# Perceiver layer in fp32 on one core: the first three tiles of cross attention in another order, with the second tile's context loaded earlier

## The chip, the cores and the metric

The kernel runs on one core of one Trainium2 chip. Time is device microseconds of one execution, and the number compared is the median of several executions. Everything is fp32. The engines in this text are PE (TensorE, matrix products; PEld is its weight load), DVE (VectorE), ACT (ScalarE), POOL (GpSimd) and SP (SyncE, which here only issues DMAs). They run side by side and meet through semaphores; each engine works off its own list of instructions strictly in the order written.

## The reference, cut to what matters

The change touches the first of three parts, a cross attention of 32 batches with 64 query rows each on a context of 1601 rows. The other two parts (causal attention, mixture of experts) are unchanged.

```
def _L0_xattn_ref(encoder_hc, decoder_hq, w_sim, b_sim, W_qv, b_qv):
    w1, w2, w3 = (w_sim[:d], w_sim[d:2 * d], w_sim[2 * d:])
    Sim = (encoder_hc @ w1)[:, :, None] + (decoder_hq @ w2)[:, None, :] + jnp.einsum('bid,bjd->bij', encoder_hc * w3, decoder_hq) + b_sim[0]
    A = jax.nn.softmax(Sim, axis=2)
    hq_hat = jnp.einsum('bij,bjd->bid', A, decoder_hq)
    Batt = jax.nn.softmax(jnp.max(Sim, axis=2), axis=1)
    hc_bar = jnp.einsum('bi,bid->bd', Batt, encoder_hc)[:, None, :]
    hc_hat = jnp.broadcast_to(hc_bar, encoder_hc.shape)
    feats = jnp.concatenate([encoder_hc, hq_hat, encoder_hc * hq_hat, encoder_hc * hc_hat], axis=-1)
    return feats @ W_qv + b_qv
...
x = x + _L0_xattn_ref(_layernorm(x, axis=-1), ctx_1024, ...)
```

## The kernel before

The 2048 rows of x are 16 tiles t of 128 rows; a tile is two batches. For each tile the context of both batches comes from memory twice: transposed, T(t), as four chunks k of two DMAs of 800.5 KB each (`load_ctx_T`, line 339), and by rows, N(t), as four groups q of two DMAs of 768 KB and a rest of two DMAs of 130 KB (`load_ctx_N`, lines 350 and 353). That is about 13.1 MB a tile. Each has one buffer only: chunk k of T(t) is issued when PE has used chunk k of T(t-1) (`sim_done`), group q of N(t) when PE has used group q of N(t-1) (`pv_done`). All loads go through SP's one queue, in the order written.

The work of one tile on PE, with the names in the code:

- `normed_T(t)` (line 1551): transposes of the normed rows. DVE makes the queries `qT` of them (`queries`, line 921).
- `similarities(t)` (line 1590), called sim(t) here: 32 matmuls in four chunks k; chunk k needs chunk k of T(t). The scores fill four banks.
- DVE takes the row maximum of the scores (`maxima`, line 930, then `diag`, line 936), ACT the exponential (line 597).
- `spread_max(t)` (line 1624) and `exp_T(t)` (line 1630): they need `diag` and the exponential.
- `attend(t)` (line 1652): 26 matmuls in groups q of N(t).
- `attended_T(t)` (line 1551), `batch_means(t)` (line 1572): of the attended rows, which DVE scales (`attended`, line 975).
- `features(t)` (lines 1602 and 1605): 8 matmuls with the middle half of `w_qv`; it waits once for `wqv_in`.
- `combined_chunk(t, k)` (line 1613), k = 0 to 3: matmuls with weights that DVE combines from the two outer quarters of `w_qv` (`combined`, line 997, which waits once for `wqv_ends_in`).

There are two orders. The *deep* order (`stage_a(t)`) does attended_T, batch_means and features of tile t-1, then spread_max and exp_T of tile t, normed_T(t+1), attend(t) with the four combined chunks of tile t-1 between its groups, and then sim(t+1). So the features of t-1 stand between sim(t) and spread_max(t). The *early* order (`early_features(t)`), used before for tiles 0 and 1, ends a tile within itself: attended_T(t), batch_means(t), features(t), then sim(t+1) with the combined chunks of tile t between its four chunks, and straight after it spread_max(t+1). Before, the deep order starts with tile 3. DVE and ACT have lists to match.

The rows of x come in groups that `TW`, `TX` and `TY` bound: row block 0 first, then 1 to TW-1 (ahead of N(0)), TW to TX-1 (after N(1)), then two more. `finish_norm` takes a group's statistics to the layer norm's factors: a chain of small DVE steps and a square root on ACT.

Of the kernel before, what the change touches and what calls it, by code (L numbers as in the profile page):

```python
# [42 lines left out]
TX = 7  # L43
TW = 3
TY = (TX + T) // 2
# [8 lines left out]
def perceiver_layer(nc, x, ctx_n, ctx_t, w1, w23, b_sim, w_qv, b_qv, wq, wk, wv, wm, b_qk, bv, bm,  # L54
# [5 lines left out]
    with ExitStack() as stack:  # L60
# [267 lines left out]
        def _(sp):  # L328
# [30 lines left out]
            sp.dma_start(X[:, 1:TW, :], x_v[:, 1:TW, :]).then_inc(x_early, 16)  # L359
            load_ctx_N(0, True)  # L360
            sp.dma_start(row_b[:, :], b_qv.partition_broadcast(P)).then_inc(rows_in, 16)
            sp.dma_start(bqkc[:, :, :], b_qk).then_inc(rows_in, 16)
# [4 lines left out]
            for t in range(1, TX - 1):  # L367
                load_ctx_T(t, False)
                if t == TX - 3:
                    sp.dma_start(X[:, TX:TY, :], x_v[:, TX:TY, :]).then_inc(x_in[0], 16)  # L370
                if t == TX - 2:
                    sp.dma_start(X[:, TY:T, :], x_v[:, TY:T, :]).then_inc(x_in[1], 16)
                load_ctx_N(t, False)
                if t == 1:
                    sp.dma_start(X[:, TW:TX, :], x_v[:, TW:TX, :]).then_inc(x_early, 16)
# [207 lines left out]
        def _(act):  # L583
# [22 lines left out]

            def after_scores(t, i, first=False, more=True, norms=None):
# [14 lines left out]
                nc.scalar.activation(ecol, smx, ACT.Exp, bias=nbmax).then_inc(bexp_ready, 1)  # L622
                if norms is not None:
                    sqrt_of_var(*norms)
                if more:
                    normed_copy(t + 1, 1 - i, first)
# [4 lines left out]

            def stage_a(t, i, more=True, norms=None):
                attended_copy(t - 1)
                exp_scores(t, False)
                after_scores(t, i, more=more, norms=norms)

            sqrt_of_var(0, 0, 1)
            normed_copy(0, 0, True)
            exp_scores(0, True)
            after_scores(0, 0, first=True, norms=(1, 1, TW))  # L640
            stage_a(1, 1)
            stage_a(2, 0, norms=(2, TW, TX))
            for t in range(3, TX - 1):
# [209 lines left out]
        def _(dve):  # L853
# [132 lines left out]

            def combined(t, k, first=False, ahead=2):

                if k > 0:
                    dve.wait_ge(wc_used, (KD - 1) * t + k)  # L990
                else:
                    dve.wait_ge(hbar_ready, t + 1)
                    dve.wait_ge(c_ready, min(t + ahead + 1, T) if isinstance(t, int) else t + ahead + 1)
# [16 lines left out]

            def early_features(t, i, first=False):
                features(t, i)
                combined(t, 0, first, ahead=1)
                other_chunks(t)
                residual_a(t)

            def stage_a(t, i, more=True):
# [5 lines left out]
                combined(t - 1, 0)  # L1023
                batch_max(t, False)
# [23 lines left out]
            attended(0, True)  # L1048
            early_features(0, 0, first=True)
            maxima(1, False)  # L1050
            norm_a(2, False)
            batch_max(1, False)
            exp_copies(1, False)
            queries(2, False)
            batch_weights(1, False)
            attended(1, False)
            early_features(1, 1)
            maxima(2, False)
            batch_max(2, False)
            exp_copies(2, False)  # L1060
            batch_weights(2, False)
            dve.wait_ge(x_early, 32)
            for t in range(TW, TX):
                row_stats(t).then_inc(stats_ready, 1)
            finish_norm(2, TX + 2, TW, TX)
            norm_a(3, False)
            queries(3, False)
            attended(2, False)
            for t in range(3, TX - 2):
# [476 lines left out]
        def _(pe):  # L1546
# [33 lines left out]

            def similarities(t, first, between=None):
                pe.wait_ge(qT_ready, KD * (t + 1))
# [3 lines left out]
                for k in range(KD):  # L1586
# [5 lines left out]
                    last.then_inc(sim_done, 1)  # L1592
                    if between is not None:
                        between(k)

# [38 lines left out]

            def attend(t, i, first=False, alone=False):

                if not first:
                    pe.wait_ge(hq_ready, t)
                for c in range(JC):
# [14 lines left out]
                    if c % 3 == 2 or c == JC - 1:  # L1654
                        last.then_inc(pv_done, 1)
                    if c % 3 == 2 and not alone:
                        combined_chunk(t - 1, 1 - i, c // 3)
# [6 lines left out]

            def early_features(t, first=False):
                attended_T(t, first)
                batch_means(t)
                features(t, first)
                similarities(t + 1, False, between=lambda k: combined_chunk(t, t % 2, k))

            def stage_a(t, i, more=True):

                attended_T(t - 1)
                batch_means(t - 1)
                features(t - 1)
# [11 lines left out]
            exp_T(0)  # L1687
            attend(0, 0, first=True, alone=True)
            normed_T(1, False)
            early_features(0, first=True)  # L1690
            spread_max(1)
            exp_T(1)
            normed_T(2, False)
            attend(1, 1, alone=True)
            early_features(1)
            spread_max(2)
            exp_T(2)
            attend(2, 0, alone=True)
            normed_T(3, False)
            similarities(3, False)  # L1700
            stage_a(3, 1)
            with pe.Fori(2, T // 2 - 1) as n:
                for i in range(2):
# [417 lines left out]
```

## Time and profile before

| | |
|---|---|
| median of 3 runs | 1434.79 us (1433.67 to 1434.84) |
| profiled execution, its own time | 1433.62 us |
| its span, first to last instruction | 1431.9 us |
| PE busy | 1368.9 us, 96% of the span |
| DVE busy | 678.1 us, 47% |
| ACT busy | 303.3 us, 21% |
| moved by DMA | 305.40 MB |
| mean granted PE clock | 0.984 of full |

The cross attention takes the first 610 us, 36 us a tile once it runs evenly. The page cuts the span into 40 slices of 35.8 us; a digit is a busy share in tenths. In the timeline views each line is a run of like instructions, with start, time to the end of the last, engine, line, what it writes and reads, the count, and in brackets how long the engine sat idle before and what ended that. A matmul of these shapes shows as two records, so `x64` at line 1590 are the 32 matmuls of sim(t). Ends of matmuls are modelled, so PE may read as busy through short waits.

### The profile page before, as it was taken

What the parts mean: (1) busy time and instruction counts of PE and PEld (TensorE: products, weight loads), DVE (VectorE), ACT (ScalarE), POOL (GpSimd) and SP (SyncE); (2) the same over time, 40 slices, a digit from 0 to 9 for tenths busy, and PEclk for the clock granted to TensorE, in tenths of its full rate; (3) what the DMA queues carried; (4) which work ended last, traced back from release to release, by engine and by line L of the source; (5) the groups of instructions that cost most, each with busy time, mean ns of one, the idle gap of its engine ahead of it and who ended that gap; (6) DMA issues with size and microseconds to landing.
All of it is one profiled execution on the core that took longest, in us unless ns stands there. A gap on an engine that the chain in (4) does not pass through costs nothing.

```text
span 1431.9 us, 20806 instructions
## 1 busy us (share of the span) xinstructions
PE 1368.9 (96%) x7264; PEld 808.1 (56%) x7265; DVE 678.1 (47%) x1251; ACT 303.3 (21%) x518; POOL 167.6 (12%) x197
## 2 busy tenths in 40 slices
PE   6988999999999999979999999999999999999996
PEld 2333444444444444358888887899884444444573
DVE  3234455544444444457777776675432222222244
ACT  2011111111111111125333334323221111111110
POOL 0100000000000000111311003004310000000065
PEclk9999999999999999989999999999999999999998
DMA  9999999999999999526000001314373322222176
GB/s 367 396 400 400 396 391 395 388 384 365 367 361 363 370 363 361 183 87 266 2 0 0 0 0 60 139 69 176 120 274 91 111 92 84 93 74 73 52 230 189
DMA packets 101534, 305.40 MB, mean 213 GB/s; under 512 B 10065, under 2 KB 30545, under 8 KB 101489
## 3 DMA queue, kind: packets, MB, share of 16 engines
q1 hardware_dynamic: 96368, 288.01, 53.7%
q0 software_dynamic: 5120, 16.78, 3.6%
q8 instruction: 30, 0.49, 0.1%
q14 instruction: 16, 0.12, 0.0%
HBM read 269.62 MB, written 35.13 MB: 213 GB/s over the span
## 4 chain that ended last, share of the span: by engine, by line
PE 46%; DVE 3%; issue 3%; POOL 2%; DMA 2%; ACT 1%; SPq 0%; POOLq 0%; DVEq 0%; ACTq 0%
PE ps L1735 11%; PE ps L2013 9%; PE ps L2000 9%; PE ps L1725 8%; PE ps L1551 3%; PE ps L1771 2%; POOL arena L571 2%; DMA arena<-w2t 1%; PE ps L1754 1%; PE ps L1743 1%; PE ps L1864 1%; POOL idx L567 1%; ACT arena L585 0%; DMA moe_in<-arena,idx 0%; PE ps L1613 0%
## 5 line engine op out<-in xcount | busy, mean ns | idle before, releaser
L585 ACT ACTIVATE arena<-ps 128x512 f32<-128x512 f32 x155 | 90.6, 597 | 608.0 <-PE ps L1551 311.8
L1652 PE MATMUL ps<-arena 128*64 128x512 f32 (+1 forms) x832 | 192.0, 597 | 0.0
L1590 PE MATMUL ps<-arena 128*64 128x512 f32 (+1 forms) x1024 | 179.9, 506 | 4.2 <-DVE arena L921 2.9
L1735 PE MATMUL ps<-split 128*128 128x256 f32 x1344 | 171.1, 287 | 1.2 <-DVE split L1092 1.2
L1735 PEld LDWEIGHTS ps<-split 128*128 128x128 f32 x1344 | 165.1, 193 | 6.4 <-issue 5.6
L997 DVE SCALAR_TENSOR_TENSOR arena<-arena,hbar 128x512 f32<-128x512 f32 x128 | 91.9, 759 | 109.3 <-PE ps L1613 105.2
L2013 PE MATMUL ps<-arena 128*128 x312 | 140.4, 592 | 1.2 <-DMA arena<-w2t 1.2
L2000 PE MATMUL ps<-arena 128*128 x312 | 140.4, 593 | 0.4 <-DVE arena L1375 0.4
L1590 PEld LDWEIGHTS ps<-arena 128*64 128x64 f32 x1024 | 66.2, 138 | 130.3 <-issue 122.6
L1652 PEld LDWEIGHTS ps<-arena 128*64 128x64 f32 (+1 forms) x832 | 58.6, 138 | 113.6 <-issue 113.2
L2013 PEld LDWEIGHTS ps<-arena 128*128 128x128 f32 x312 | 59.0, 190 | 75.2 <-issue 75.2
L1725 PE MATMUL ps<-split 128*128 128x512 f32 x384 | 96.0, 399 | 0.7 <-DVE arena L1153 0.7
L1375 DVE STREAM_TRANSPOSE arena<-arena 128x512 uint32<-128x512 uint32 x39 | 27.7, 711 | 134.6 <-PE ps L2000 116.2
L930 DVE TENSOR_REDUCE small<-ps 128x1 f32<-128x1601 f32 x16 | 29.2, 1823 | 127.4 <-PE ps L1590 127.4
L2000 PEld LDWEIGHTS ps<-arena 128*128 128x128 f32 x312 | 56.2, 190 | 56.8 <-issue 56.8
L1725 PEld LDWEIGHTS ps<-split 128*128 128x128 f32 x384 | 69.8, 188 | 17.9 <-issue 2.7
L1551 PE MATMUL ps<-ident,arena 128*128 128x128 f32 x368 | 56.3, 287 | 23.4 <-DVE arena L884 12.2
L495 POOL COPY arena<-arena 128x512 f32<-128x512 f32 x16 | 10.8, 673 | 517.7 <-PE ps L1572 512.4
L1613 PE MATMUL ps<-arena 128*64 128x512 f32 x256 | 66.9, 601 | 4.6 <-DVE arena L997 4.6
L1481 DVE COPY arena<-ps 128x512 f32<-128x512 f32 x39 | 27.0, 691 | 85.6 <-PE ps L2013 85.6
L1725 PE MATMUL ps<-split_ws,split 128*128 128x512 f32 x288 | 67.2, 392 | 0.0
L1551 PEld LDWEIGHTS ps<-ident,arena 128*128 128x128 f32 x368 | 44.0, 147 | 30.7 <-DVE arena L975 11.7
(175 smaller groups left out, 1549.9 us busy)
## 6 DMA issues: line engine op xcount, KB each, us to landing
arena<-ctx_t SPq DMA_DIRECT2D x128, 800.5 KB, 13.7
arena<-ctx_n SPq DMA_DIRECT2D x128, 768.0 KB, 9.2
moe_in<-arena SPq DMA_DIRECT2D x3, 3328.0 KB, 24.0
arena<-moe_in SPq DMA_DIRECT2D x156, 64.0 KB, 1.9
moe_out<-arena SPq DMA_DIRECT2D x39, 256.0 KB, 2.1
arena<-w1t SPq DMA_DIRECT2D x1, 7168.0 KB, 23.1
arena<-ctx_n SPq DMA_DIRECT2D x32, 130.0 KB
arena<-w2t SPq DMA_DIRECT2D x4, 1024.0 KB
```

What stands on the lines that cost most here:

```text
L571: nc.gpsimd.indirect_dma_start(y01[k][i], None, moe_out, bass.IndirectOffsetOnAxis(ap=idx[k][i][:, :], axis=0)).then_inc(y01_in[i], 16)
L585: return nc.scalar.activation(o, i, ACT.Copy)
L930: v.reduce_max(smax, ps[:, 0:4, :].rearrange("p a b -> p (a b)")[:, 0:J], AX).then_inc(max_ready, 1)
L997: v.scalar_tensor_tensor(Wc[:, h, :], w_qv_sb[:, 3 * KD + k, :], hbar[:, k, h:h + 1], w_qv_sb[:, k, :], ALU.mult, ALU.add).then_inc(wc_rea ...
L1551: last = nc.tensor.transpose(dst[:, P * k:P * (k + 1)], src[:, P * k:P * (k + 1)], ident[:, :])
L1590: last = mm(bank(n)[S * h:S * (h + 1), 0:w], qT[:, k, S * h:S * (h + 1)], ctxT[h][:, k, at_j:at_j + w], start=(k == 0), stop=(k == KD - 1))
L1613: last = mm(bank(5)[r, :], F1[i][:, k, r], Wc[:, h, :], start=False, stop=(k == KD - 1))
L1652: last = mm(bank(7)[S * h:S * (h + 1), :], ET[0:w, c, S * h:S * (h + 1)], ctxN[h][0:w, c, :], start=(c == 0), stop=(c == JC - 1))
L1725: last = mm(dst, lhs[a][:, k, :], rhs[b][:, k, :], start=(k + i == 0), stop=(k == n - 1 and i == 2))
L1735: last = mm(dst[:, 2 * P * m:2 * P * (m + 1)], w[a][:, k, c], tokens[b][:, k, :], start=(k + i == 0), stop=(k == KD - 1 and i == 2))
L2000: m1 = mm(bank(2), xgT[:, k, :], w1_sb[:, bass.ds(e, 1), k, :].rearrange("p o f -> p (o f)"), start=(k == 0), stop=(k == KD - 1))
L2013: m2 = mm(bank(3), interT[:, k, :], w2_of(e, k), start=(k == 0), stop=(k == KD - 1))
```

## The change

Three things are changed, together.

1. **Loads.** T(1) is issued right after N(0), ahead of `row_b`, `bqkc` and the three DMAs of `w_qv` (4 MB in all). Before, it came behind them.
2. **Order.** `early_features` is gone on PE and DVE. After attend(0) and normed_T(1), sim(1) follows at once, and the deep order runs from tile 1 on.
3. **Rows of x.** TW is 4 instead of 3: the early group is row blocks 1 to 3 (ahead of N(0)), the next is 4 to 6 and is issued after N(2), where before 3 to 6 was issued after N(1). The square root of that group on ACT and the norm on DVE come after stage_a(2).

```
-TW = 3
+TW = 4
...
             load_ctx_T(0, True, 1, KD)
             sp.dma_start(X[:, 1:TW, :], x_v[:, 1:TW, :]).then_inc(x_early, 16)
             load_ctx_N(0, True)
+            load_ctx_T(1, False)
             sp.dma_start(row_b[:, :], b_qv.partition_broadcast(P)).then_inc(rows_in, 16)
...
             for t in range(1, TX - 1):
-                load_ctx_T(t, False)
+                if t > 1:
+                    load_ctx_T(t, False)
...
                 load_ctx_N(t, False)
-                if t == 1:
+                if t == 2:
                     sp.dma_start(X[:, TW:TX, :], x_v[:, TW:TX, :]).then_inc(x_early, 16)
...
-            after_scores(0, 0, first=True, norms=(1, 1, TW))
+            after_scores(0, 0, first=True)
             stage_a(1, 1)
-            stage_a(2, 0, norms=(2, TW, TX))
+            stage_a(2, 0)
+            sqrt_of_var(2, TW, TX)
...
-            early_features(0, 0, first=True)
-            maxima(1, False)
-            norm_a(2, False)
...
-            early_features(1, 1)
...
+            stage_a(1, 1, second=True)
+            stage_a(2, 0)
             dve.wait_ge(x_early, 32)
             for t in range(TW, TX):
                 row_stats(t).then_inc(stats_ready, 1)
             finish_norm(2, TX + 2, TW, TX)
-            norm_a(3, False)
-            queries(3, False)
-            attended(2, False)
...
-            attend(0, 0, first=True, alone=True)
+            attend(0, 0, first=True)
             normed_T(1, False)
-            early_features(0, first=True)
-            spread_max(1)
-            exp_T(1)
-            normed_T(2, False)
-            attend(1, 1, alone=True)
-            early_features(1)
-            spread_max(2)
-            exp_T(2)
-            attend(2, 0, alone=True)
-            normed_T(3, False)
-            similarities(3, False)
-            stage_a(3, 1)
-            with pe.Fori(2, T // 2 - 1) as n:
+            similarities(1, False)
+            stage_a(1, 1, second=True)
+            with pe.Fori(1, T // 2 - 1) as n:
                 for i in range(2):
                     stage_a(2 * n + i, i)
```

How the instructions stand. First SP's queue from the early rows of x on, before:

```order
L359 DMA arena<-x 128x2x512
L350 DMA arena<-ctx_n 128x1536 x8
L353 DMA arena<-ctx_n 65x512 x2
L361 DMA row_b<-b_qv 128x512
L362 DMA bqkc<-b_qk 128x8
L364 DMA arena<-w_qv 128x8x512
L365 DMA arena<-w_qv 128x4x512
L366 DMA arena<-w_qv 128x4x512
L339 DMA arena<-ctx_t 128x1601 x8
```

and in the change, where the line numbers differ by one or two:

```order
L359 DMA arena<-x 128x3x512
L350 DMA arena<-ctx_n 128x1536 x8
L353 DMA arena<-ctx_n 65x512 x2
L339 DMA arena<-ctx_t 128x1601 x8
L362 DMA row_b<-b_qv 128x512
L363 DMA bqkc<-b_qk 128x8
L365 DMA arena<-w_qv 128x8x512
L366 DMA arena<-w_qv 128x4x512
L367 DMA arena<-w_qv 128x4x512
```

The eight DMAs of T(1) have passed the five of the features' weights and biases; N(1) follows in both. Next PE's list from attend(0) on, before (line 1652 attend, 1551 transposes, 1572 batch means, 1602 and 1605 features, 1590 similarities, 1613 combined chunks):

```order
L1652 MATMUL ps<-arena 64x512 x26
L1551 MATMUL ps<-ident,arena 128x128 x8
L1572 MATMUL ps<-arena 128x128 x4
L1602 MATMUL ps<-arena 128x512 x4
L1605 MATMUL ps<-arena 128x512 x4
L1590 MATMUL ps<-arena 64x512 x6
L1590 MATMUL ps<-arena 64x65 x2
L1613 MATMUL ps<-arena 64x512 x2
...
L1624 MATMUL ps<-arena,ones 128x128
L1630 MATMUL ps<-ident,arena 128x128 x12
```

and in the change (there 1633 is attend, 1534 the transposes, 1573 similarities, 1555 batch means, 1583 and 1586 features, 1605 spread_max, 1611 exp_T, 1594 combined chunks):

```order
L1633 MATMUL ps<-arena 64x512 x26
L1534 MATMUL ps<-ident,arena 128x128 x4
L1573 MATMUL ps<-arena 64x512 x6
L1573 MATMUL ps<-arena 64x65 x2
...
L1534 MATMUL ps<-ident,arena 128x128 x4
L1555 MATMUL ps<-arena 128x128 x4
L1583 MATMUL ps<-arena 128x512 x4
L1586 MATMUL ps<-arena 128x512 x4
L1605 MATMUL ps<-arena,ones 128x128
L1611 MATMUL ps<-ident,arena 128x128 x12
```

Batch means and features of tile 0 have moved from before sim(1) to between sim(1) and spread_max(1); the combined chunks of tile 0 now stand within attend(1). Last DVE's list after it has scaled the attended rows of tile 0, before (979 and 984 features, 997 combined weights, 930 row maximum, 945 batch maximum):

```order
L979 COPY hbar<-ps 128x8
L984 TENSOR_TENSOR arena<-arena 128x512
L997 SCALAR_TENSOR_TENSOR arena<-arena,hbar 128x512 x8
L1007 TENSOR_TENSOR arena<-arena,ps 128x512
L887 BN_STATS stats<-arena 128x6
L930 TENSOR_REDUCE small<-ps 128x1
```

and in the change (933 row maximum, 982 and 987 features, 887 the normed rows of the next tile, 1000 combined weights, 948 batch maximum, 967 a copy of the transposed exponentials):

```order
L933 TENSOR_REDUCE small<-ps 128x1
...
L982 COPY hbar<-ps 128x8
L987 TENSOR_TENSOR arena<-arena 128x512
L887 TENSOR_SCALAR arena<-arena,rstd,nmr 128x512
L916 SCALAR_TENSOR_TENSOR arena,small<-arena,row_a 128x512
L1000 SCALAR_TENSOR_TENSOR arena<-arena,hbar 128x512 x2
L948 TENSOR_REDUCE small<-ps 64x1 x2
L950 TENSOR_SCALAR small<-small 128x1
L967 COPY arena<-ps 128x512
```

The row maximum of tile 1 now comes ahead of tile 0's features, and the first combined weights, which wait for the last of `w_qv`, have the batch maximum and the copies of tile 1 queued behind them.

## Rows read from the trace of the kernel before

**Rows 1.** The page, 40 slices: busy share of the DMA engines, GB/s moved.
```profile
DMA  9999999999999999526000001314373322222176
GB/s 367 396 400 400 396 391 395 388 384 365 367 361 363 370 363 361 183 87 266 2 0 0 0 0 60 139 69 176 120 274 91 111 92 84 93 74 73 52 230 189
```

**Rows 2.** Stretches: length, busy PE, PEld, DVE, ACT, POOL; PE clock, DMA share, GB/s.
```profile
82.00:116.00 34.00, 33.15 (x158) 12.51 (x154) 9.43 (x16) 1.19 (x2) 2.79 (x2) 1.00 1.02 401
116.00:126.00 10.00, 5.65 (x23) 3.81 (x23) 5.44 (x13) 4.10 (x10) 0.00 (x0) 0.66 1.02 354
...
320.00:360.00 40.00, 40.00 (x207) 16.86 (x205) 16.43 (x33) 5.05 (x11) 1.84 (x2) 1.00 0.98 370
```

**Rows 3.** Timeline of PE, tiles 0 to 3 (start, length, what, idle before).
```profile
40.04 0.14 PEld L1652 LDWEIGHTS ps<-arena 128*64 128x64 f32 x2 [0.43 <-DMA arena<-ctx_n]
...
43.86 0.65 PE L1551 MATMUL ps<-ident,arena 128*128 128x128 f32 x4
46.91 1.11 PE L1551 MATMUL ps<-ident,arena 128*128 128x128 f32 x4 [2.39 <-DVE arena L975]
...
64.51 2.92 PE L1590 MATMUL ps<-arena 128*64 128x512 f32 x16 [0.15 <-DMA arena<-ctx_t]
...
68.42 2.92 PE L1590 MATMUL ps<-arena 128*64 128x512 f32 x16
...
76.08 0.49 PE L1624 MATMUL ps<-arena,ones 128*128 128x128 f32 x2 [3.88 <-DVE arena L936]
...
119.98 0.80 PE L1624 MATMUL ps<-arena,ones 128*128 128x128 f32 x2 [3.88 <-DVE arena L936]
...
138.17 11.00 PE L1590 MATMUL ps<-arena 128*64 128x512 f32 x64 [1.46 <-DVE arena L921]
```

**Rows 4.** Timeline of PE in the even part, tiles 3 to 5, deep order.
```profile
159.58 2.79 PE L1652 MATMUL ps<-arena 128*64 128x512 f32 x12
162.21 1.03 PE L1613 MATMUL ps<-arena 128*64 128x512 f32 x4
...
174.23 10.95 PE L1590 MATMUL ps<-arena 128*64 128x512 f32 x64
...
210.24 10.95 PE L1590 MATMUL ps<-arena 128*64 128x512 f32 x64
```

**Rows 5.** DMA issues by line: issue ns, first to last start; time to landing.
```profile
L364 SPq DMA_DIRECT2D arena<-w_qv x1: 1606/1606/1606, 26.2 to 26.2; - x1
DMA to landing us min/median/max: 21.0/21.0/21.0
...
L366 SPq DMA_DIRECT2D arena<-w_qv x1: 2923/2923/2923, 37.7 to 37.7; - x1
DMA to landing us min/median/max: 15.0/15.0/15.0
...
L339 SPq DMA_DIRECT2D arena<-ctx_t x2: 795/1389/1983, 82.1 to 84.1; - x2
DMA to landing us min/median/max: 19.5/20.0/20.5
...
L339 SPq DMA_DIRECT2D arena<-ctx_t x2: 633/800/968, 115.3 to 116.0; - x2
DMA to landing us min/median/max: 19.5/20.6/21.7
...
L339 SPq DMA_DIRECT2D arena<-ctx_t x3: 452/587/1106, 219.2 to 222.1; - x3
DMA to landing us min/median/max: 19.9/20.5/21.5
```

**Rows 6.** PE groups by form, from 10 to 16 us, then from 19 to 23 us.
```profile
L1590 PE MATMUL ps<-arena 128*64 128x512 f32 x14 | 6.2, 1032 | 1.5 <-DVE arena L921 1.5
...
L1590 PE MATMUL ps<-arena 128*64 128x512 f32 x14 | 3.5, 606 | 1.0 <-DMA arena<-ctx_t 1.0
```

**Rows 7.** Timeline of DVE at the end of sim(3).
```profile
149.22 1.82 DVE L930 TENSOR_REDUCE small<-ps 128x1 f32<-128x1601 f32 x1 [10.19 <-PE ps L1590]
```

More of the change, by code:

```diff
@@ L605, in normed_copy, with after_scores @@
                 copy(F1[i].rearrange("p a b -> p (a b)"), bank(4)).then_inc(F1_ready, 1)
-            def after_scores(t, i, first=False, more=True, norms=None):
+            def after_scores(t, i, first=False, more=True):
                 for g in (0, 2):
@@ L622, in after_scores @@
                 nc.scalar.activation(ecol, smx, ACT.Exp, bias=nbmax).then_inc(bexp_ready, 1)
-                if norms is not None:
-                    sqrt_of_var(*norms)
+                if first:
+                    sqrt_of_var(1, 1, TW)
                 if more:
@@ L630, in attended_copy, with stage_a @@
                 copy(F2.rearrange("p a b -> p (a b)"), bank(5)).then_inc(F2_ready, 1)
-            def stage_a(t, i, more=True, norms=None):
+            def stage_a(t, i, more=True):
                 attended_copy(t - 1)
                 exp_scores(t, False)
-                after_scores(t, i, more=more, norms=norms)
+                after_scores(t, i, more=more)
             sqrt_of_var(0, 0, 1)
@@ L985, in features, with combined @@
                                 F2.rearrange("p a b -> p (a b)"), ALU.mult).then_inc(F3_ready, 1)
-            def combined(t, k, first=False, ahead=2):
+            def combined(t, k, first=False):
                 if k > 0:
@@ L992, in combined @@
                     dve.wait_ge(hbar_ready, t + 1)
-                    dve.wait_ge(c_ready, min(t + ahead + 1, T) if isinstance(t, int) else t + ahead + 1)
+                    dve.wait_ge(c_ready, min(t + 3, T) if isinstance(t, int) else t + 3)
                 if first:
@@ L1009, in residual_a, with stage_a @@
                 row_stats(t).then_inc(stats_ready, 1)
[L1011 to L1017, printed above, removed]
+            def stage_a(t, i, second=False, more=True):
                 maxima(t, False)
@@ L1022, in stage_a @@
                     norm_a(t + 1, False)
-                combined(t - 1, 0)
+                combined(t - 1, 0, second)
                 batch_max(t, False)
@@ L1048, in _ @@
             attended(0, True)
-            early_features(0, 0, first=True)
-            maxima(1, False)
-            norm_a(2, False)
[L1052 to L1056, printed above, removed]
-            early_features(1, 1)
[L1058 to L1061, printed above, removed]
+            stage_a(1, 1, second=True)
+            stage_a(2, 0)
             dve.wait_ge(x_early, 32)
@@ L1579, in attended_T, with similarities @@
                 transposes(bank(5), hq).then_inc(hqT_done, 1)
-            def similarities(t, first, between=None):
+            def similarities(t, first):
                 pe.wait_ge(qT_ready, KD * (t + 1))
@@ L1592, in similarities @@
                     last.then_inc(sim_done, 1)
-                    if between is not None:
-                        between(k)
             def features(t, first=False):
@@ L1633, in exp_T, with attend @@
                         last.then_inc(et_done, 1)
-            def attend(t, i, first=False, alone=False):
+            def attend(t, i, first=False):
                 if not first:
@@ L1655, in attend @@
                         last.then_inc(pv_done, 1)
-                    if c % 3 == 2 and not alone:
+                    if c % 3 == 2 and not first:
                         combined_chunk(t - 1, 1 - i, c // 3)
@@ L1663, in normed_T_b, with stage_a @@
                 transposes(bank(i), h1[i]).then_inc(h1T_done, 1)
[L1665 to L1673, printed above, removed]
+            def stage_a(t, i, second=False, more=True):
+                attended_T(t - 1, second)
                 batch_means(t - 1)
-                features(t - 1)
+                features(t - 1, second)
                 spread_max(t)
```

## The prediction

> **What bounds the kernel now.** I read the page's slices first: over the first sixteen the DMA engines are at nine tenths or more, at 360 to 400 GB/s [rows 1]. PE is at nine as well, so the question is which of the two ends last, and where. The stretches tell: from 82 to 116 us the DMA share is 1.02 at 401 GB/s, and only at 320 us does it fall to 0.98 at 370 [rows 2]. Until then transfers are never idle, so they are behind what the free buffers would allow, and a landing can only come earlier if bytes ahead of it in the queue go away. Then the timeline of PE: in the even part sim(4) starts at 174.23 and sim(5) at 210.24, 36.0 us apart, with no idle time, and a sim takes 10.95 [rows 4]; so from the end of a sim to the start of the next is 25.1. There PE is the bound: a tile is 13.1 MB, and at 401 GB/s that is 32.7 us. Before 138 us PE has holes: 2.39 for the scaled rows, twice 3.88 for `diag` straight after a sim, 1.46 for the queries, and smaller ones [rows 3], and after such holes the clock is low (0.66 from 116 to 126 us, [rows 2]). The first three tiles thus have spare PE time, but the transfers set a floor under them.
>
> One rule of the Trainium skill would settle the case otherwise. The rows show 401 GB/s over 34 us [rows 2]. The page "DMA: Bandwidth & Descriptors", section "Where 436 GB/s comes from", says that for transfers from HBM to SBUF the HBM side, about 358 GB/s for a core, binds. By that a tile would take an estimated 36.6 us, transfers would bound all sixteen and no order of PE could gain; the trace goes above it, so I go by the trace.
>
> **The change, part by part.** *Order, on PE alone.* The matmuls are the same ones. After attend(0) and normed_T(1), which ends at 44.5 [rows 3], the queries cost 1.5 as at 138.17, and sim(1) could start at 46.0. With 36.0 a tile, sim(3) would start at 118.0 instead of 138.17: 20 us less. This is the gain if all data were there. The two holes of 3.88 vanish because batch means and features of the tile before (over 7 us) stand between the sim and spread_max, as in the even part, where DVE's maximum runs under them. The hole of 2.39 is covered by sim(1).
>
> *Loads: T(1).* The last large piece of N(0) lands at about 40.0, where a weight load of attend(0) waited for it [rows 3]. The last of `w_qv` lands at 37.7 + 15.0 = 52.7, its middle half at 26.2 + 21.0 = 47.2 [rows 5]. So biases and `w_qv` hold the queue 12.7 us, the part up to the middle half 7.2. T(1)'s chunks 2 and 3 were computed as they landed, at 64.5 and 68.4 [rows 3]; they are 3.9 us apart (1.64 MB, so 418 GB/s). In the change T(1) has 12.7 us less ahead of it, and 0.6 more for the extra row block of x (256 KB at 418 GB/s). Its last chunk lands at 68.4 - 12.7 + 0.6 = 56.3, the others at 44.5, 48.4 and 52.4. A chunk's matmuls take 2.8, so sim(1) ends at 59.1 instead of 57.0. Issue does not hold it: T(1) needs only that sim(0) has used the buffers, over by 25.5, while N(0) still streams until 40.
>
> *Loads: the weights.* The middle half of `w_qv` lands at 56.3 + 7.2 = 63.5, the ends at 69.0. PE wants it for features(0) at about 60.6 (sim(1) end, transposes, batch means), so there is a new hole of 3 us, features end at 70.5 and attend(1) starts at about 73. On DVE the first combined weights wait until 69.0; behind them stand batch maximum and copies of tile 1, which PE's exp_T feeds only from 70.7, so that wait costs nothing. POOL's bias add waits for `row_b`, landing before 60, ahead of the copy that it owes at 60.6.
>
> *Loads: N(1) and T(2).* The bytes ahead of N(1) are the same plus one row block of x, so it lands 0.6 later than before. T(2)'s last chunk landed at 84.1 + 20.5 = 104.6 [rows 5]; before it stood a group of four row blocks of x, 1 MB or 2.5 us, which now comes after N(2). So T(2)'s last chunk lands at 104.6 + 0.6 - 2.5 = 102.7, and its chunks come 3.9 apart, from 91.0. N(1) was complete about 15.7 + 2.5 before 104.6, at 86.4, now 87.0; attend(1) and its combined chunks run at 3.8 a group against a landing every 3.9 and end near 90. So sim(2) starts at 91.0, is paced by the transfers, and ends at 102.7 + 2.8 = 105.5. On PE alone it would have ended at 93: 12 us of the 20 are lost here, and this is the step that sets the gain.
>
> *T(3) and later.* From there 36.0 a tile: sim(3) ends at 141.5. T(3)'s last chunk lands at 116.0 + 21.7 = 137.7 [rows 5], unchanged, since three row blocks of x are behind N(2) and one ahead of N(0), together the same bytes; that floor would be 140.5, just under. N(2), 1.9 earlier than before, is wanted later than it lands. Before, sim(3) ended at 149.1. The gain is 149.1 - 141.5 = 7.6 at sim(3). Is it kept? Later tiles are wanted 7.6 earlier while landing no earlier. The tightest I found is T(6): its last chunk lands at 222.1 + 21.5 = 243.6 at most [rows 5], and sim(6), at 210.24 + 36.0, wants it at 254.5. 10.9 of slack against 7.6: no wait. From 320 us on transfers wait for buffers, so they move with PE, and what follows the cross attention waits for PE.
>
> *Norms.* The statistics and the norm of the second group of rows now come on DVE after attended(2), some 4 us of work, against a wait of 10.19 for the end of a sim at that point [rows 7]: hidden, with 5 us to spare until maxima(3). ACT's square root goes with it, and is over before attended_T(2) needs ACT.
>
> **Sum**, against the profiled execution's own 1433.62: minus 7.6 gives 1426.0. That run is 1.2 below the median of the three, 1434.79; from the median it is 1427.2, which I give.
>
> **What the traces do not show** is PE's clock in the new stretch. Half speed shows as 1032 ns for a matmul of 592 to 606 [rows 6]. What speaks against trouble: in sim(0), from 19 to 23 us, PE waited 1.0 us for a chunk of the same size and its matmuls took 606 ns, having sped up from 1032 while it was paced by the same transfers. So waits of 1.1 us in sim(2) should leave the clock up. The hole of 3 us ahead of features(0) is like those of 2.39 and 3.88 and should bring half speed; the features then last up to 3 us longer, which N(1)'s landings mostly hide. A low stretch after 105.5 would not be hidden: 3.4 us cost 1.5, the 6.8 of 116 to 126 (0.34 of 10 us, doubled) [rows 2] cost 2.9. Below, the bound is nothing.
>
> The Trainium skill's page "TensorE: Matmul & The Clock Gate", section "HAM oscillation — how this bites in real kernels", describes kernels whose every group of matmuls starts at half speed since a DMA wait precedes it; sim(2) has that form. The trace's sim(0) disagrees, so the rule gets a small chance, as the last rival.
>
> **The rivals.** *A, one or two low-clock stretches after 105.5*: 1.5 to 2.9 later, 1428.7 to 1430.1. For it: before, each hole over 2 us had one. Against it: none is expected there.
> *B, T(2) lands earlier than I read* and T(3) is the floor: sim(3) ends at 140.5, a gain of 8.6, 1426.2.
> *C, transfers don't bind* and the PE sum holds: 1414.6. Only if the queue had gaps before; a share of 1.02 says no.
> *D, most is lost*: a low clock from 105.5 on and T(2) landing 2 later, because the weights' rows, moved next to N(1), slow its transfer; 1431.9 to 1434. Nothing shows it.
> *E, slower: PE at half speed through the paced stretch.* Attend(1) with its chunks takes 14.7, sim(2) 10.95; at 1032 against 592 they take 25.6 and 19.1. From a start at 79, sim(2) ends at 123.7 and the kernel at 1445. It decides where half speed adds over 12 us of matmul time (4.5 of slack in sim(2), plus 7.6), so if it lasts for some 28 us on end; the longest seen here is 6.8.
>
> **Chances.** Forecast (1425.5 to 1428.5) 0.55, A 0.22, B 0.07, C 0.03, D 0.08, E 0.05. Forecast, A and B hold 0.84; the range is 1425.0 to 1430.8. A change within 0.2%, 2.9 us, can't be told from none here: faster 0.87, same 0.08, slower 0.05.
>
> **What would show it.** Right: no idle time of 3.88 before spread_max of tiles 1 and 2; a hole of about 3 us before features(0), ended by `w_qv`; four starts about 3.9 apart in sim(2), the last at 102.7; sim(3) from 130.6 to 141.5; none idle after. Wrong: the last chunk of T(2) at another time than 101.5 to 104; PE waiting for T(4) to T(8); matmuls of 1032 ns after 105; sim(3) following sim(2) by other than 36.0.

## The result and the profile after

The changed kernel takes 1422.49 us (median of 4 executions, 1419.65 to 1425.44) against 1434.36 for the kernel before (4, 1433.67 to 1434.84). The ratio is 0.9917, with a 95% interval of 0.9896 to 0.9939: 0.8% faster, 11.9 us. The forecast was 7.6 us, 1427.2 with a range from 1425.0: right in direction, too small in size, and the time is outside the range. Over all sessions, this one included, 22 executions of the changed kernel have a mean of 1423.0 and 56 of the kernel before one of 1433.7, so the gain is better put at 10.7 us.

The page of the changed kernel (its profiled execution took 1425.44), span and the slices that answer to [rows 1]:

```profile
span 1423.7 us, 20826 instructions
...
DMA  9999999999999999336000001414373322222176
GB/s 366 393 398 394 394 394 399 402 401 392 380 368 366 364 367 367 139 106 250 1 0 0 0 0 61 149 60 178 119 274 94 116 90 88 89 73 74 52 229 192
```

What is new is that transfers stay above 390 GB/s from the second slice through the tenth, before only through the seventh: PE asks for its data earlier, and the transfers are behind for longer. Now PE's timeline for tiles 0 to 3, against [rows 3] (line 1534 transposes, 1573 similarities, 1583 features, 1633 attend):

```profile
45.37 0.66 PE L1534 MATMUL ps<-ident,arena 128*128 128x128 f32 x4
47.48 5.61 PE L1573 MATMUL ps<-arena 128*64 128x512 f32 x32 [1.46 <-DVE arena L924]
...
57.47 2.92 PE L1573 MATMUL ps<-arena 128*64 128x512 f32 x16 [1.01 <-DMA arena<-ctx_t]
...
63.74 3.67 PE L1583 MATMUL ps<-arena 128*128 128x512 f32 x8 [1.87 <-DMA arena<-w_qv]
...
73.42 2.79 PE L1633 MATMUL ps<-arena 128*64 128x512 f32 x12 [0.50 <-DMA arena<-ctx_n]
...
85.99 2.79 PE L1633 MATMUL ps<-arena 128*64 128x512 f32 x12 [1.49 <-DMA arena<-ctx_n]
...
91.12 2.91 PE L1573 MATMUL ps<-arena 128*64 128x512 f32 x16 [0.61 <-DMA arena<-ctx_t]
94.95 2.92 PE L1573 MATMUL ps<-arena 128*64 128x512 f32 x16 [0.92 <-DMA arena<-ctx_t]
98.86 2.92 PE L1573 MATMUL ps<-arena 128*64 128x512 f32 x16 [1.00 <-DMA arena<-ctx_t]
103.22 2.92 PE L1573 MATMUL ps<-arena 128*64 128x512 f32 x16 [1.44 <-DMA arena<-ctx_t]
...
131.20 10.96 PE L1573 MATMUL ps<-arena 128*64 128x512 f32 x64
```

The two waits of 3.88 are gone. From 45 us on every wait that is left, but for the queries, ends with a transfer: features(0) waits for `w_qv` until 63.74 (forecast 63.5), sim(2) is computed chunk by chunk as T(2) lands, from 91.12 (91.0) to the last chunk at 103.22 (102.7), and sim(3) starts at 131.20 (130.6), where before it was 138.17: 7.0 us. The stretches (columns as in [rows 2]) show PE's clock on this way:

```profile
46.00:106.00 60.00, 49.12 (x244) 19.80 (x243) 18.54 (x38) 6.93 (x13) 3.10 (x3) 1.00 1.03 399
106.00:142.00 36.00, 36.00 (x185) 15.38 (x180) 19.68 (x44) 6.54 (x13) 1.84 (x2) 1.00 1.02 394
```

The clock is whole throughout the paced stretch, and from 106 on PE is never idle until the end of the cross attention. The norm on DVE was hidden as forecast: DVE's wait for the end of sim(3), 10.19 before [rows 7], is still 5.55.

```profile
142.26 1.83 DVE L933 TENSOR_REDUCE small<-ps 128x1 f32<-128x1601 f32 x1 [5.55 <-PE ps L1573]
```

So the profile shows the 7.6 that was forecast as 7.0, and the median says 11.9. That gap was the first thing to explain.

To see where time goes after sim(3), the matmuls of two profiles can be laid side by side by their order, since the same 7264 records are there. Both kernels were profiled several times for this (below). Mean of nine profiles of the kernel before and of six of the changed one, in us; the borders are times of the kernel before's first profile:

| stretch | before | changed | difference |
|---|---|---|---|
| start to sim(3) | 139.65 (138.1 to 140.9) | 131.18 (130.5 to 131.7) | -8.5 |
| to 605, rest of cross attention | 466.9 | 466.9 | 0.0 |
| to 641, its last tile and the change to attention | 35.65 | 36.35 | +0.7 |
| to 870, attention | 229.0 | 229.0 | 0.0 |
| to 924, its end | 53.73 | 52.02 | -1.7 |
| to 1100, shared experts | 175.7 | 175.1 | -0.6 |
| to 1380, experts | 279.7 | 279.7 | 0.0 |
| to 1400 | 19.66 | 18.13 | -1.5 |
| to the end | 31.31 | 33.02 | +1.7 |
| span | 1431.3 | 1421.4 | -9.9 |

The three dense stretches, to 605, to 870 and to 1380, agree within 0.1 us in all fifteen profiles. PE never waits in the first and the third, and in the second only at its start, for 0.7 and 1.2 us. All scatter sits in the other stretches, which have the holes. From sim(3)'s start to the end the spans are 1288.0 to 1293.7 before and 1288.8 to 1292.5 in the changed kernel. Their means differ by 1.4, which so few profiles do not set clear of that scatter; the 8.5 is clear of it.

### The profile page after: what moved, and what is told of

The parts are those of the page before. It is cut to its first block, busy times and chain, and to the rows that moved or that the text cites. A ratio compares the mean times of both kernels' runs of the same rounds, so it can differ in the third digit from the quotient of the medians.

```text
span 1423.7 us, 20826 instructions
## 1 busy us (share of the span) xinstructions
PE 1364.4 (96%) x7264; PEld 804.4 (57%) x7265; DVE 677.8 (48%) x1251; ACT 303.2 (21%) x518; POOL 164.5 (12%) x197
## 4 chain that ended last, share of the span: by engine, by line
PE 48%; DVE 3%; issue 2%; POOL 2%; DMA 1%; ACT 1%; POOLq 0%; SPq 0%; DVEq 0%; ACTq 0%
PE ps L1700 11%; PE ps L1965 9%; PE ps L1978 9%; PE ps L1690 9%; PE ps L1534 3%; PE ps L1736 2%; POOL arena L573 1%; PE ps L1719 1%; PE ps L1708 1%; PE ps L1829 1%; DMA arena<-moe_out,idx 1%; POOL idx L569 1%; ACT arena L587 0%; PE ps L1594 0%; DMA moe_in<-arena,idx 0%
## 5 line engine op out<-in xcount | busy, mean ns | idle before, releaser
L1583 PE MATMUL ps<-arena 128*128 128x512 f32 x128 | 59.3, 607 | 1.9 <-DMA arena<-w_qv 1.9
```

What stands on the lines that cost most here:

```text
L1583: mm(bank(5), F2[:, k, :], w_qv_sb[:, KD + k, :], start=(k == 0), stop=False)
```

## Experiments

**Is the floor set by T(2)'s landing?** Two kernels change only what is ahead of it in the queue. The first puts the group of three row blocks back:

```
                 load_ctx_N(t, False)
-                if t == 2:
+                if t == 1:
                     sp.dma_start(X[:, TW:TX, :], x_v[:, TW:TX, :]).then_inc(x_early, 16)
```

> One size changed: the group of three row blocks of x (768 KB, 1.9 us at 418 GB/s) is issued after N(1), ahead of T(2), instead of after N(2). Theory 'floor' (the landing of T(2)'s last chunk sets the end of sim(2), and all later tiles follow 36.0 apart): the last chunk is computed from 105.1 instead of 103.2, sim(3) ends at 144.0 instead of 142.1, and the kernel is 1.9 us slower than the changed kernel. Rival 'PE or DVE sets it' (the hole ahead of the features, or the waits within attend(1)): nothing moves, 0 us.

Measured: 1425.14 median (6 executions), ratio to before 0.9940 (0.9926 to 0.9955), 2.6 above the changed kernel timed beside it (1422.55; 1.9 was expected). Its PE timeline:

```profile
93.95 2.91 PE L1573 MATMUL ps<-arena 128*64 128x512 f32 x16 [2.45 <-DMA arena<-ctx_t]
...
105.62 2.92 PE L1573 MATMUL ps<-arena 128*64 128x512 f32 x16 [1.01 <-DMA arena<-ctx_t]
133.60 10.95 PE L1573 MATMUL ps<-arena 128*64 128x512 f32 x64
```

The last chunk is at 105.62; in the changed kernel's profile from the same session it is at 103.71, and sim(3) at 131.69. Both moved by 1.9, which is 768 KB at 418 GB/s.

The second leaves two thirds of N(1)'s large groups out, so what it computes is not the reference's result:

```
-                            sp.dma_start(ctxN[h][:, n * q:n * (q + 1), :],
-                                         main[:, n * q:n * (q + 1), :]).then_inc(ctxN_in[q], 16)
+                            w = 1 if isinstance(t, int) and t == 1 else n
+                            sp.dma_start(ctxN[h][:, n * q:n * q + w, :],
+                                         main[:, n * q:n * q + w, :]).then_inc(ctxN_in[q], 16)
```

> N(1) is loaded only to a third (one of three columns of each large group; attend(1) then reads rows of tile 0 for the rest, so its output is not the reference's): 4.2 MB fewer ahead of T(2), 10 us. Theory 'floor': T(2) is no longer late, sim(2) starts when attend(1) ends, about 88, and ends at 99; sim(3) ends at 135, 7 us before the changed kernel's, and the kernel is 7 us faster, since T(3) lands earlier by the same 10 us. Rival 'transfers don't bind': sim(3) ends at 142 as in the changed kernel.

Measured: 1415.13 (4 executions), 7.4 below the changed kernel. Its PE timeline (line 1574 is the similarities):

```profile
87.25 10.96 PE L1574 MATMUL ps<-arena 128*64 128x512 f32 x64
...
123.28 10.95 PE L1574 MATMUL ps<-arena 128*64 128x512 f32 x64
```

Sim(2) runs through in 10.96 without a wait, and sim(3) starts 8.4 earlier; features(0) still wait 1.87 for `w_qv`. Together they settle that step: T(2)'s landing is the floor of the first three tiles, and what moves it moves sim(3), and the kernel by about as much (1.9 and 2.6, 8.4 and 7.4), until PE is the bound.

**What is the early T(1) worth, and can it stand alone?** One kernel takes it back and keeps the rest:

```
             load_ctx_N(0, True)
-            load_ctx_T(1, False)
...
             for t in range(1, TX - 1):
-                if t > 1:
-                    load_ctx_T(t, False)
+                load_ctx_T(t, False)
```

> One part undone: T(1) again behind biases and w_qv, the deep order and the groups of x as in the change. Sim(1) then waits for T(1): its last chunk is computed from about 69 and ends at 72, features end at 80.5, attend(1) runs from 82.5 to 97, sim(2) from 97 to 108 on PE's pace, T(2) landing at 103. Theory 'floor': sim(2) ends at 108 instead of 106, sim(3) at 144, so the early T(1) is worth only 2 to 3 us of the gain, and this kernel is still 5 us faster than the kernel before. Rival 'the early T(1) is the gain': it is as slow as the kernel before.

Measured: 1426.48 (4 executions), 3.9 above the changed kernel and 8.1 below the kernel before, ratio 0.9940 (0.9925 to 0.9956). Its PE timeline (line 1571 is the similarities):

```profile
58.20 7.08 PE L1571 MATMUL ps<-arena 128*64 128x512 f32 x32 [12.30 <-DMA arena<-ctx_t]
...
97.83 10.95 PE L1571 MATMUL ps<-arena 128*64 128x512 f32 x64
...
133.84 6.42 PE L1571 MATMUL ps<-arena 128*64 128x512 f32 x36
```

Sim(1) waits 12.30 for T(1), yet sim(3) starts only 2.2 later than in the changed kernel's profile of the same session (131.69): sim(2), from 97.83, no longer waits for T(2) and ends at 108.8, where the paced one ends at 106.6. Most of the gain is thus the order, with the rows of x placed as in the change, and 2 to 4 us of it are the early T(1). The order with the rows of x where they were before was not run.

The other kernel has the kernel before's order and only the early T(1):

```
             load_ctx_N(0, True)
+            load_ctx_T(1, False)
...
             for t in range(1, TX - 1):
-                load_ctx_T(t, False)
+                if t > 1:
+                    load_ctx_T(t, False)
```

> One part alone: T(1) ahead of biases and w_qv, with the order and the groups of x of the kernel before. Features(0) then waits for the middle half of w_qv until 63 us (before: 49.5) and sim(1) with its four combined chunks runs after it, from 70 to 86 us (before: 57 to 72), attend(1) until 106, sim(2) with its chunks until 130, attend(2) until 149. Theory 'floor and order belong together': sim(3) starts at 150 to 153, the kernel is 12 to 15 us slower than before, 1447 to 1450. Rival 'the early T(1) helps by itself': sim(3) starts no later than 138, and the kernel is not slower.

Measured: 1446.79 (4 executions) against 1432.4 for the kernel before in that session, ratio 1.0102 (1.0085 to 1.0119): 14.4 slower. Its PE timeline (line 1604 features, 1626 spread_max, 1592 similarities):

```profile
64.14 6.29 PE L1604 MATMUL ps<-arena 128*128 128x512 f32 x8 [13.84 <-DMA arena<-w_qv]
...
92.11 0.49 PE L1626 MATMUL ps<-arena,ones 128*128 128x128 f32 x2 [3.88 <-DVE arena L938]
...
154.04 11.01 PE L1592 MATMUL ps<-arena 128*64 128x512 f32 x64 [1.46 <-DVE arena L923]
```

In that order features(0) stands ahead of sim(1), and all of PE's work waits for `w_qv`. After that wait of 13.84 the first matmuls of features(0) also run at half speed, in 6.29 where the changed kernel needs 3.67. Sim(3) starts a microsecond later than the 150 to 153 expected. The load order and the instruction order have to match; the early T(1) alone is a loss.

**Is the hole ahead of the features free?** The last variant puts T(1) between the two parts of `w_qv`:

```
             load_ctx_N(0, True)
-            load_ctx_T(1, False)
             sp.dma_start(row_b[:, :], b_qv.partition_broadcast(P)).then_inc(rows_in, 16)
...
             sp.dma_start(w_qv_sb[:, KD:3 * KD, :], w_qv_v[:, KD:3 * KD, :]).then_inc(wqv_in, 16)
+            load_ctx_T(1, False)
             sp.dma_start(w_qv_sb[:, 0:KD, :], w_qv_v[:, 0:KD, :]).then_inc(wqv_ends_in, 16)
```

> T(1) stands between the two parts of w_qv: biases and the middle half first, then T(1), then the outer quarters; all else as in the change, and the bytes ahead of N(1) and T(2) are the same. Features(0) has its weights when sim(1) ends, so the hole of 1.9 to 3 us ahead of it is gone, but sim(1) waits for T(1) and ends at 67 instead of 61. Theory 'floor': attend(1) starts at 77 instead of 74, ends at 92, and sim(2) is still paced by T(2): sim(3) starts at 131 to 132 and the kernel is within 1 us of the changed kernel. Rival 'PE's work ahead of attend(1) counts': sim(3) starts 5 us later.

Measured: 1423.98 (4 executions), ratio 0.9928 (0.9910 to 0.9946), within the changed kernel's own scatter. Its PE timeline:

```profile
53.31 10.89 PE L1573 MATMUL ps<-arena 128*64 128x512 f32 x48 [7.45 <-DMA arena<-ctx_t]
64.97 2.92 PE L1573 MATMUL ps<-arena 128*64 128x512 f32 x16 [0.77 <-DMA arena<-ctx_t]
69.20 3.66 PE L1583 MATMUL ps<-arena 128*128 128x512 f32 x8
92.94 5.66 PE L1573 MATMUL ps<-arena 128*64 128x512 f32 x32
...
103.51 2.92 PE L1573 MATMUL ps<-arena 128*64 128x512 f32 x16 [0.99 <-DMA arena<-ctx_t]
...
131.50 3.72 PE L1573 MATMUL ps<-arena 128*64 128x512 f32 x20
```

The features have no wait and start 5.5 later than in the changed kernel; sim(3) starts 0.3 later. What PE does before attend(1) can slip by 5 us for nothing.

**Where is the rest of the gain?** The changed kernel again, unaltered, in five rounds:

> The changed kernel again, unaltered, for the part of the gain that its first profile doesn't hold: 8.2 us there, while two further executions were 13 to 15 us below the kernel before. Theory 'clock': what is over 7 us comes from stretches at half PE clock that fall differently from execution to execution after 599 us; then span and granted clock of the executions lie on one line, about 0.5 us of span for each 1 us of low clock (0.001 of mean clock is 1.4 us of low clock, 0.7 us of span), and times spread from 1419 to 1426 without a step. Rival 'transfers': some executions had T(2) land earlier; then the profile shows sim(3) ending at 137 instead of 142 in a fast execution, and the mean clock doesn't tell the spans apart.

Measured: 1422.55 (5 executions) against 1434.61 (11), ratio 0.9916 (0.9903 to 0.9928). Sim(3) starts at 131.69, 0.5 later than in the first profile, though the span, 1422.1, is 1.6 shorter. So no early landing of T(2) makes the fast executions, and the rival 'transfers' falls. 'Clock' holds only roughly: the executions' mean clocks, 0.989 to 0.992, do not order their times. What was still unknown was how typical the kernel before's one profile is. Three further ones:

> The kernel before, unaltered, a second profiled execution (its first started sim(3) at 138.2 us, span 1431.9). What is open: the changed kernel's two profiles start sim(3) at 131.2 and 131.7, 7.0 and 6.5 us earlier, and keep that to 605 us, but the medians are 12.1 apart. Theory 'first part': the kernel before starts sim(3) later than 138.2 in most executions, 140 to 144, because the matmuls after its holes run at half clock for longer or shorter, and my one profile was a lucky one. Theory 'later part': sim(3) starts at 138 within 0.6 in each, and the other 5 us lie after 605 us, in the stretches at half clock after holes that both kernels have (at 613, 900, 1385, 1415 us).

> The kernel before, a third profiled execution. 'First part': sim(3) starts at 140 to 144. 'Later part': at 138 within 0.6, and the shift of 2 to 3 us against other executions arises at 613 to 634 or at 890 to 905 us.

> The kernel before, a fourth profiled execution, the same two readings: sim(3) at 140 to 144, or at 138 within 0.6.

Measured: sim(3) starts at 139.96, 138.40 and 140.49, after a first 138.17. So neither reading is right alone, and 'first part' is nearer: the start varies by over 2 us, and my one profile was at the short end. Then both kernels side by side on one chip, the changed one in five rounds (after_3), with one more profile of it (after_4) and two of before (before_5, before_6):

> The changed kernel, unaltered, on the chip on which two executions of the kernel before are profiled beside it. By the profiles so far sim(3) starts at 138.2, 140.0, 138.4 and 140.5 us in the kernel before (mean 139.3) and at 131.2 and 131.7 in the changed one: 7.8 us. The medians taken side by side are 12 apart. Theory 'start of before': what lacks lies in the kernel before's first 140 us, whose holes are followed by more or less half clock; beside this kernel's median its profiles show sim(3) at 141 or later. Theory 'later part': from sim(3)'s start to the end the changed kernel needs less than the kernel before, by 3 us or more (so far: 1290.4 to 1292.5 against 1287.9 to 1293.7, no difference). Theory 'the medians of before on that chip were high': here the medians are 8 to 10 apart.

> The kernel before, a fifth profile, beside the changed kernel. 'Start of before': sim(3) from 141 us or later; 'later part': sim(3) from 138 to 140.5 and then 1292 us or more to the end.

> The changed kernel, a further profile. Both theories: sim(3) from 131 to 132, since the landing of T(2) sets it and not the clock; 'later part': 1289 us or less from there to the end.

> The kernel before, a sixth profile, with the same two readings as the fifth.

Measured: 1423.90 (5 executions) against 1433.83 (9), ratio 0.9933 (0.9918 to 0.9947), 9.9 us. Sim(3) starts at 131.19 and 130.45 in the changed kernel, at 139.83 and 138.10 in the one before; the rest of the span is 1289.1 and 1290.4 against 1293.0 and 1290.8. Sim(3) is not at 141, and the later part differs by under 3 on the mean, so the first two theories fail as stated. The third one's reading came, medians 8 to 10 apart: part of the first 12 was the scatter of the medians. Last, three more of before (before_7 to before_9) and two of the changed kernel (after_5, and after_6 in five rounds):

> The kernel before, a seventh profile. Theory 'scatter': sim(3) starts between 138 and 141, and the rest of the span is 1288 to 1294, around 1292; with the eighth and ninth the mean of the whole goes up towards the 1432.0 of all executions. Theory 'later part': the rest is 1292 or more in each of the new profiles of before, and 1290 or less in each of the changed kernel.

> The changed kernel, a fifth profile: sim(3) starts at 130.5 to 131.7. 'Scatter': the rest lies anywhere in 1288 to 1293. 'Later part': 1290 or less.

> The kernel before, an eighth profile, the same readings as the seventh.

> The changed kernel, a sixth profile and five rounds against the kernel before. 'Scatter': the rest after sim(3)'s start is anywhere in 1288 to 1293, and the medians are 9 to 12 apart. 'Later part': 1290 or less.

> The kernel before, a ninth profile. 'Scatter': rest anywhere in 1288 to 1294. 'Later part': 1292 or more.

Measured: after_6 1423.46 (6 executions) against 1434.08 (11), ratio 0.9928 (0.9911 to 0.9945). Sim(3) of before at 140.36, 140.87 and 140.67, of the changed kernel at 131.25 and 131.30. Rest of the span: 1293.0, 1291.7 and 1292.8 against 1290.1 and 1288.8. The medians are 10.6 apart. All of this lies where 'scatter' has it. 'Later part' is missed, by 0.3 in before_8 and by 0.1 in after_5, which is too little to rule out that a small difference is real.

Much of what makes the first part of the kernel before long or short is visible in its stretches. The same ten microseconds around the first wait of 3.88, in the first profile and then in before_7:

```profile
75.00:85.00 10.00, 8.14 (x39) 5.08 (x41) 5.45 (x19) 4.45 (x10) 0.00 (x0) 0.83 1.03 368
```

```profile
75.00:85.00 10.00, 7.51 (x30) 4.94 (x31) 6.39 (x19) 4.46 (x10) 0.00 (x0) 0.66 1.02 368
```

A clock of 0.83 against 0.66: half speed (1.2 GHz) for 3.4 us in the one, for 6.8 in the other. The nine profiles fall in two groups by it. The three with 3.4 us (the first, before_3 and before_6) start sim(3) at 138.10 to 138.40, the six with 6.8 us at 139.83 to 140.87. In before_7:

```profile
140.36 10.03 PE L1590 MATMUL ps<-arena 128*64 128x512 f32 x56 [1.46 <-DVE arena L921]
```

This stretch is not all of it. The wait itself ends at 76.08 in the first profile and at 76.79 on the mean of nine, so 0.7 of the 1.5 us by which the first profile is early are there already. Of the six late profiles, four (before_2, 5, 7 and 9) have 10.2 us of half speed ahead of that wait instead of 6.8. The other two (before_4 and before_8) have no more of it than the early ones, but sim(1) waits for chunks of T(1), up to 1.03 and 1.52 us: there the transfers were late, not the clock.

In the changed kernel the stretches at half speed that occur between 46 and 69 us cost nothing. In after_5 there were two of them, behind attend(0) and behind the hole for `w_qv`:

```profile
46.00:106.00 60.00, 51.73 (x243) 20.64 (x243) 18.26 (x38) 6.94 (x13) 3.10 (x3) 0.94 1.03 401
```

and sim(3) started at 131.25, against 131.20 with the clock whole.

The second piece is at the end of attention. Before_7, then after_6, at the same matmuls:

```profile
892.25 0.63 PE L1551 MATMUL ps<-ident,arena 128*128 128x128 f32 x4 [1.60 <-DVE arena L884]
893.57 0.66 PE L1551 MATMUL ps<-ident,arena 128*128 128x128 f32 x4 [0.69 <-DVE arena L884]
...
900.33 1.11 PE L1551 MATMUL ps<-ident,arena 128*128 128x128 f32 x8 [2.02 <-DVE arena L884]
902.99 1.12 PE L1551 MATMUL ps<-ident,arena 128*128 128x128 f32 x4 [1.54 <-DVE arena L1180]
903.89 1.92 PE L1743 MATMUL ps<-ident,arena 128*128 128x128 f32 x8
```

```profile
882.98 1.31 PE L1534 MATMUL ps<-ident,arena 128*128 128x128 f32 x8 [1.53 <-DVE arena L887]
...
890.12 1.11 PE L1534 MATMUL ps<-ident,arena 128*128 128x128 f32 x8 [1.74 <-DVE arena L887]
892.78 0.66 PE L1534 MATMUL ps<-ident,arena 128*128 128x128 f32 x4 [1.54 <-DVE arena L1163]
893.27 1.04 PE L1708 MATMUL ps<-ident,arena 128*128 128x128 f32 x8
```

After the last hole, 1.54 in both, the same transposes take 1.12 in the one and 0.66 in the other. All nine profiles of the kernel before have a stretch at half speed near there (seven at 900, two at 892 us), but only two of the changed kernel's six. In the changed kernel alone the stretch to 924 takes 51.5 us without it and 52.9 and 53.4 with it. But the clock is not all of the 1.7 us of the table, for the holes ahead differ too. The wait of 0.69 is in all nine profiles of the kernel before and in none of the changed kernel's, and the one of 2.02, in the seven, is 1.74 or 1.75 in all six. With half speed at the same place (the seven, and after) the changed kernel is 0.7 us shorter. The change touches no instruction there; the waits end with DVE's norms, and why those come earlier was not tested. In the kernel before sim(3) starts 12.3 to 13.0 us after the end of the last low stretch in all nine profiles, while in the changed kernel the transfers place it; whether that is why the later holes meet the clock otherwise was not tested either. Both stay open. So does what the 0.8 us are between the profiles' 9.9 and the 10.7 of all executions: the profiled ones are few, and single executions of either kernel scatter by 1.6 to 1.8 us (one standard deviation).

## Why the prediction was right in its steps and too small in its size

*That the transfers set a floor under the first three tiles, and PE is the bound after them*: right; moving 768 KB ahead of T(2) moved sim(3) by 1.9, and from 106 us on PE does not wait. By the rule of the Trainium skill (page "DMA: Bandwidth & Descriptors", section "Where 436 GB/s comes from") that about 358 GB/s binds there would have been no gain. The changed kernel, on one core, moves 399 over 60 us, so the trace disagrees.

*Order on PE alone, 20 us*: not reached, as forecast. With two thirds of N(1) left out sim(3) starts at 123.28, 15 us ahead of before and not 20, since T(1) and `w_qv` still land when they do.

*Landings*, forecast and in brackets measured: `w_qv` at 63.5 (63.74), T(2)'s last chunk at 102.7 (103.22), T(1)'s last at 56.3 (57.47, the worst miss, without effect), the hole ahead of the features 3 us (1.87). That hole was to bring half speed; it did in two of the six profiles (after_4 and after_5), and cost nothing there.

*From there 36.0 a tile, kept to the end of cross attention*: right, with no wait of PE from 106 us on; T(6) did not bind.

*The clock in the paced stretch stays up*: right, 1.00. The rule of the Trainium skill on DMA waits that leave every group of matmuls at half speed (page "TensorE: Matmul & The Clock Gate", section "HAM oscillation — how this bites in real kernels") describes waits of about 3 to 5 us. Those ahead of sim(2)'s chunks were 0.6 to 1.4, so sim(2) had less of that form than I said and doesn't test the rule. The long waits for a transfer in the experiments (7.45, 12.30 and 13.84 us) were each followed by matmuls at half speed, which agrees with it. Rivals A, C, D and E fell; B (T(3) as the floor) did too, sim(3) having ended at 142.2, 0.7 later than forecast.

*Norms hidden*: right.

**The step that failed is the last one, the sum**: "The gain is 149.1 - 141.5 = 7.6 at sim(3)" takes the start of the difference from one execution of the kernel before. Its end was right to 0.6. The start was not a constant: over nine profiles sim(3) of the kernel before starts at 139.65 on the mean, 1.5 later than in the one I had. About half of that comes after the first wait of 3.88, with 6.8 instead of 3.4 us of half speed behind it in six profiles; the other half is there before it, from half speed behind earlier holes and, in two profiles, from T(1) landing later. The changed kernel waits for T(2) whatever came before (its scatter at sim(3) is 0.4 us against 1.1), so it gains this mean as well: 8.5 in place of 7.6. I had weighed low clock only as a loss in the changed kernel (rival A), never as a cost in the kernel before that would go away.

The two means, 1433.7 and 1423.0, place the rest. The changed kernel's mean is 4.2 below the forecast. Of these 1.1 are the base: the median of three, 1434.79, from which I subtracted, was high, and 1426.0 from the profiled execution would have been nearer. The start of the difference gives 0.9. "What follows the cross attention waits for PE" left out that the later holes differ in clock and in length: 1.4 in the profiles' mean, not clear of their scatter. The last 0.8 no profile places. It was luck that the first profile of the changed kernel took 1425.44, near 1426.0: its span after sim(3), 1292.5, is the longest of the six. The range had the same gap as the sum: its lower end, 1425.0, is 1.2 below rival B's 1426.2, with no room for the mean of before nor for the scatter of 1.6 to 1.8 us of an execution.

## What to carry to other kernels

Where transfers are never idle, find the transfer whose landing ends a chain last, and count the bytes ahead of it in the queue: that gave the new start of sim(3) to 0.6 us, and the experiments with the changed order moved it by about what was computed. An order that asks for data earlier is worth only what that landing allows, and it needs the loads in the same order; the load order alone cost 14 us. And a gain is a difference of two executions, each with its own luck of the clock: with one profile of the kernel before, take the holes on its path, price the half clock after each, and the transfers' own scatter, as a range, and remember that a change that hides those holes behind a later landing wins their mean, not the value of the one trace.

## What the runs showed of the hardware

- After a hole of the same length at the same place, PE's clock fell for 3.4 us, for 6.8 us or not at all, from one execution of the same program to the next. In the kernel before the first wait of 3.88 was followed by 3.4 in three profiles and by 6.8 in six, the wait of 2.39 by 3.4 in seven, by 6.8 in one and by none in one (before_8). The wait of 1.54 near 890 us of the changed kernel was followed by half speed in two profiles and by full in four.
- Five or six waits of 0.16 to 1.6 us for transfers between 72 and 104 us left the clock at 2.4 GHz in all six profiles of the changed kernel. Waits of 7.45, 12.30 and 13.84 us for a transfer (t1_between, t1_behind, t1_only, one profile each) were followed by half speed, granted clock 0.57 from 46 to 62 us of t1_behind.
- Stretches in which PE never waits repeat to 0.1 us over 466 us; the scatter of the kernel's time comes from a few holes.
- Half speed costs nothing where PE would wait for the next landing anyway: two stretches of 3.4 us ahead of sim(2) in after_5 left sim(3) at 131.25.
